# Residual tokens turned on VectorE through HBM, group statistics moved to the second stage, and both ends of the kernel put in a new order

## The reference

```
x1 = x + proj(softmax(q k^T / 16) v),   q, k, v = 1x1 convolutions of group_norm(x, 8 groups)
t  = tokens(x1)                                        # (1024, 256)
a  = ln(t);  u = a / |a|
t2 = t + softmax((u u^T)^2) a                          # second attention, symmetric scores
y  = ln(t2) @ sign(W - mean(W)) * mean|W| + bias
out = t2 + round(clip(y, -1, 1) * 7) / 7               # back to (256, 32, 32)
```

## Time and profile before

| | us |
|---|---|
| median of three runs | 1703.02 (1702.33 to 1707.27) |
| the profiled execution | 1704.85 |
| its span | 1703.1 |
| TensorE matmul busy | 1652.5 (97%) |
| VectorE busy | 1381.0 (81%) |
| ScalarE busy | 989.0 (58%) |
| GpSimd busy | 717.7 (42%) |
| DMA queue, share of 16 engines | 51.1%, 259.48 MB |

### The profile page before, as it was taken

How to read it: one execution, slowest core, us unless ns; L and a number is a source line. 1 busy time by engine, 2 the same in 40 slices (tenths; PEclk the granted TensorE clock), 3 DMA queues, 4 the chain that set the end, 5 groups by cost and what they waited for, 6 DMA issues and landing times.

```text
span 1703.1 us, 33336 instructions
## 1 busy us (share of the span) xinstructions
PE 1652.5 (97%) x10994; PEld 1511.6 (89%) x10994; DVE 1381.0 (81%) x2687; ACT 989.0 (58%) x1586; POOL 717.7 (42%) x1078
## 2 busy tenths in 40 slices
PE   7899999999999999999999999999999999999996
PEld 6798899989899898998989999898998989989895
DVE  7779688787878879788797887878788797887875
ACT  3565655657555565655657566565655656556562
POOL 1262534625345253543625346253542635336251
PEclk9999999999999999999999999999999999999998
DMA  4545546355454554545455463554545545564541
GB/s 144 154 121 170 147 152 184 124 172 158 150 165 143 172 156 151 156 152 185 135 160 161 149 184 124 175 160 146 166 149 174 161 137 155 156 186 107 173 131 56
DMA packets 218750, 259.86 MB, mean 153 GB/s; under 512 B 30176, under 2 KB 188256, under 8 KB 218720
## 3 DMA queue, kind: packets, MB, share of 16 engines
q1 hardware_dynamic: 218720, 259.48, 51.1%
HBM read 138.81 MB, written 120.59 MB: 152 GB/s over the span
## 4 chain that ended last, share of the span: by engine, by line
PE 36%; issue 25%; POOL 15%; DVE 13%; ACT 6%; DMA 2%; SPq 1%; POOLq 1%; DVEq 0%; ACTq 0%
PE wide L466 13%; DVE neg_max L1134 4%; POOL root_pair L1470 3%; PE turn L629 3%; PE turn L631 3%; PE turn L630 3%; PE narrow L629 3%; PE narrow L631 3%; PE narrow L630 3%; PE narrow L466 3%; DVE prob L1206 2%; POOL val L1489 2%; DMA e_scratch<-x_norm 1%; ACT expo L887 1%; DVE x_norm L1143 1%
## 5 line engine op out<-in xcount | busy, mean ns | idle before, releaser
L466 PE MATMUL wide<-xn_hi,prob 128*128 128x512 f32 x1024 | 296.0, 395 | 1.8 <-ACT expo L823 1.1
L823 ACT ACTIVATE expo<-wide,neg_max 128x1024 f32<-128x1024 f32 x128 | 142.9, 1116 | 234.2 <-DVE neg_max L1134 234.2
L466 PEld LDWEIGHTS wide<-xn_hi,prob 128*128 128x128 f32 x1024 | 187.6, 188 | 43.0 <-ACT expo L823 1.2
L1143 DVE STREAM_TRANSPOSE x_norm<-expo 128x1024 f32<-128x1024 f32 x112 | 139.4, 1244 | 51.2 <-ACT expo L823 48.7
L830 ACT ACTIVATE prob<-e_back 128x1024 fp32r<-128x1024 f32 x112 | 118.2, 1055 | 81.1 <-DMA e_back<-e_scratch 80.7
L1513 POOL TENSOR_TENSOR carrier_p<-ones 128x1 f32<-128x1 f32 x60 | 11.7, 195 | 363.5 <-DVE y_sb L1250 361.0
L1497 POOL TENSOR_TENSOR prob<-expo,prob 128x128 fp32r<-128x128 f32 (+6 forms) x112 | 146.7, 1321 | 36.0 <-DVE prob L1183 36.0
L466 PE MATMUL wide<-xn_lo,prob 128*128 128x512 f32 x512 | 160.7, 394 | 0.0
L1134 DVE TENSOR_REDUCE neg_max<-wide 128x1 f32<-128x1024 f32 x128 | 154.3, 1206 | 6.3 <-PE wide L466 6.2
L559 PE MATMUL wide<-prob 128*128 128x256 f32 x512 | 150.3, 294 | 9.0 <-DVE prob L1148 9.0
L1148 DVE TENSOR_TENSOR prob<-e_back,prob 128x1024 fp32r<-128x1024 f32 x112 | 136.0, 1214 | 20.8 <-ACT prob L830 20.3
(11 more groups left out here) (183 smaller groups left out, 5143.2 us busy)
## 6 DMA issues: line engine op xcount, KB each, us to landing
e_scratch<-x_norm SPq DMA_DIRECT2D x112, 512.0 KB, 3.6
e_back<-e_scratch SPq DMA_DIRECT2D x448, 128.0 KB, 3.0
x_raw<-in_x SPq DMA_DIRECT2D x32, 512.0 KB, 3.7
e_back<-in_x SPq DMA_DIRECT2D x64, 256.0 KB, 5.0
out<-y_sb SPq DMA_DIRECT2D x64, 256.0 KB, 3.1
ln_scratch<-x_norm SPq DMA_DIRECT2D x30, 512.0 KB, 3.0
expo<-ln_scratch SPq DMA_DIRECT2D x120, 128.0 KB, 2.9
e_scratch<-x_norm SPq DMA_DIRECT2D x32, 448.0 KB, 2.6
```

Of the source, the lines that this page charges most:

```text
L466: mm = pe.matmul(o, lhsT, r, start=first and i == 0, stop=last and i == len(parts) - 1)
L823: act.activation(expo[:, n % DEEP], wide[n % 2][:, :], ACT.Exp, bias=neg_max[:, n:n + 1], accum_out=row_sum1[:, n:n + 1]).then_inc(e1_made, 1)
L1143: dve.transpose(e_turned[:, n % 2].rearrange("p (q n t) -> p n q t", q=SQ, n=NT), expo[:, n % DEEP].rearrange("p (n q t) -> p n q t", q=SQ ...
```

## The change: what it does

The tokens of the image before no longer go through TensorE in the loop. VectorE turns the squares of `tok` into the space of `ln2` (free by then), SP sends them to a new scratch tensor and fetches them back into the same space, and `output` adds them from there, behind rows 3 and 4 of the second stage. The stores move with it into SP's `second`. The next image's group statistics move from the first to the second stage on all engines. `unit_rows(3)` on ScalarE goes ahead of `square2(3)`. At the start the loads, the first weights, `weight_means` and `signs` are put in another order; at the end `product2(NT - 2)`, `turn_ln2(f, 1)` and `quantise(f, 0)` are. The core of the diff:

```
+        tok_squares = [ln2[:, HT * hf:HT * (hf + 1), :].rearrange("p n c -> p (n c)") for hf in range(2)]
 SP
+            def send_tok(f, hf):
+                sp.wait_ge(tok_turned, 2 * f + hf + 1)
+                sp.dma_start(tok_scratch[hf], tok_squares[hf]).then_inc(tok_written[hf], 16)
+            def fetch_tok(f, hf):
+                sp.wait_ge(tok_written[hf], 16 * (f + 1))
+                back = tok_squares[hf].rearrange("p (q f) -> p q f", q=SQ)
+                for c in range(SQ):
+                    sp.dma_start(back[c * Q:(c + 1) * Q], tok_in[hf, c]).then_inc(tok_landed[hf], 16)
             def second(b, f):
                 send2(b, 0)
+                if f is not None:
+                    store(f, 0)
                 fetch2(b, 0)
                 send2(b, 1)
+                if f is not None:
+                    store(f, 1)
                 send2(b, 2)
...
                 if f is not None:
-                    store(f, 0)
-                    store(f, 1)
+                    for hf in range(2):
+                        send_tok(f, hf)
+                    for hf in range(2):
+                        fetch_tok(f, hf)
 TensorE, front
-                if more:
-                    pe.wait_ge(v_made, 4 * b + 4)
-                    group_means(b + 1)
...
                 scores1(b, 4)
-                if more:
-                    group_vars(b + 1)
-                if f is not None:
-                    pe.wait_ge(y_made, 4 * f + 4)
-                    turn_t(f, 0)
                 product1(b, 0)
                 scores1(b, 5)
-                if f is not None:
-                    pe.wait_ge(out_made, 2 * f + 1)
-                    turn_t(f, 1)
-                if more:
-                    pe.wait_ge(gn_var, b + 2)
                 product1(b, 1)
...
                 scores2(b, 6)
+                if more:
+                    group_means(b + 1)
                 scores2(b, 7)
                 scores2(b, 8)
+                if more:
+                    group_vars(b + 1)
 TensorE, last image
-            for n in range(2, NT - 2):
+            for n in range(2, NT - 1):
                 product2(f, n)
             pe.wait_ge(sq2_made, NP * f + NP)
             turn_ln2(f, 0, LAST)
-            product2(f, NT - 2)
             product2(f, NT - 1)
             ffn(f, 0, LAST)
+            turn_ln2(f, 1, LAST)
             turn_t(f, 0, LAST)
-            turn_ln2(f, 1, LAST)
             ffn(f, 1, LAST)
 ScalarE, front
                 layer_norm1(b, 3)
+                unit_rows(b, 3)
                 square2(b, 3)
                 exp2(b, 3)
-                unit_rows(b, 3)
 VectorE
+            def tok_turn(f, hf):
+                dve.wait_ge(t2_made, NT * f + HT * (hf + 1))
+                for k in range(KC):
+                    last = dve.transpose(
+                        tok_squares[hf].rearrange("p (c k n t) -> p k n c t", c=SQ, k=KC, t=Q)[:, k],
+                        tok[:, HT * hf:HT * (hf + 1), tile(k)].rearrange("p n (c t) -> p n c t", t=Q))
+                last.then_inc(tok_turned, 1)
+            def output(f, hf):
+                dve.wait_ge(tok_landed[hf], 16 * SQ * (f + 1))
+                dve.wait_ge(q_made, 2 * f + hf + 1)
+                y = y_sb[:, hf].rearrange("p k (q f) -> p k q f", q=SQ)
+                dve.tensor_tensor(y, tok_squares[hf].rearrange("p (q k f) -> p k q f", q=SQ, k=KC), y, ALU.add
+                                  ).then_inc(out_made, 1)
 VectorE, front (gn_sums, gn_deviation, gn_variance and output are gone from the first stage)
                 row_max(b, 4)
+                if f is not None:
+                    tok_turn(f, 0)
                 e1_turn(b, 4)
...
                 e1_turn(b, 6)
+                if f is not None:
+                    tok_turn(f, 1)
                 row_max(b, 7)
...
                 cosT_lo(b, 1)
+                if more:
+                    gn_sums(b + 1, 0)
                 residual1(b, 7)
                 cosT_lo(b, 2)
+                if f is None:
+                    signs()
                 e2_turn(b, 1)
+                if more:
+                    gn_sums(b + 1, 1)
...
                 e2_turn(b, 3)
+                if f is not None:
+                    output(f, 0)
                 cosT_lo(b, 3)
                 e2_hi(b, 4)
                 e2_turn(b, 4)
+                if f is not None:
+                    output(f, 1)
                 e2_hi(b, 5)
                 e2_turn(b, 5)
+                if more:
+                    gn_deviation(b + 1)
                 e2_hi(b, 6)
                 e2_turn(b, 6)
+                if more:
+                    gn_variance(b + 1)
 VectorE, last image
             clip(f, 0)
+            quantise(f, 0)
             ln2T_lo_last(f, 1, LAST)
-            quantise(f, 0)
-            output(f, 0, LAST)
+            output_last(f, 0, LAST)
```

More of the change, by code:

```diff
@@ L445, in _ @@
             reload_quads(1)
-            second(0)
+            second(0, None)
             with sp.Fori(1, B - 1) as b:
@@ L450, in _ @@
                 reload_quads(b + 1)
-                second(b)
+                second(b, b - 1)
             front(B - 1, B - 2)
-            second(B - 1)
+            second(B - 1, B - 2)
             store(B - 1, 0)
@@ L467, in three, with query_weights @@
                 return mm
+            def query_weights(k):
+                pe.wait_ge(qkv_loaded, 16)
+                for o in range(KC):
+                    mm = pe.matmul(wide[0][:, k * C:(k + 1) * C], qkv_ld[:, o, tile(k)], qkv_ld[:, KC + o, :],
+                                   start=o == 0, stop=o == KC - 1)
+                if k == KC - 1:
+                    mm.then_inc(prep_pe, 1)
             def prepare():
-                pe.wait_ge(qkv_loaded, QKV_LOADS)
+                pe.wait_ge(proj_loaded, 16)
                 for j in range(KC):
@@ L475, in prepare @@
                 mm.then_inc(prep_pe, 1)
[L477 to L480, removed]
                 pe.wait_ge(gn_var, 1)
+                pe.wait_ge(qkv_b_loaded, 16)
                 for k in range(KC):
@@ L683, in ffn, with turn_t @@
                 mm.then_inc(y_up, 1)
-            def turn_t(f, hf, places=PLACES):
+            def turn_t(f, hf, places):
                 for k in range(KC):
@@ L698, in front @@
                 if f is None:
-                    pe.wait_ge(prep_dve, 8)
+                    weight_sums()
                 queries(b, 1)
                 if f is None:
-                    pe.wait_ge(prep_dve, 12)
+                    pe.wait_ge(prep_dve, 10)
                 else:
@@ L1010, in back @@
                     layer_norm2(b, n)
-            act.wait_ge(prep_pe, 1)
+            normalise(0, 0, False)
+            act.wait_ge(prep_pe, 2)
             act.activation(projT, turn[:, 0:KC * C].rearrange("p (t c) -> p t c", c=C), ACT.Copy
                            ).then_inc(prep_act, 1)
-            for k in range(KC):
-                normalise(0, k, False)
-                norm_hi(0, k, False)
+            norm_hi(0, 0, False)
+            normalise(0, 1, False)
+            norm_hi(0, 1, False)
             act.wait_ge(ffn_loaded, FFN_LOADS)
             act.activation(abs_w, ffn_ld, ACT.Abs, accum_out=w_sum[:, 1:2]).then_inc(prep_act, 1)
-            act.wait_ge(prep_dve, 4)
+            act.wait_ge(prep_dve, 5)
             front(0, None, True)
@@ L1259, in quantise, with output_last @@
                                   ).then_inc(q_made, 1)
-            def output(f, hf, places=PLACES):
-                dve.wait_ge(tT_up, 2 * f + hf + 1)
+            def output(f, hf):
[4 more added lines that the diff above has]
+                                  ).then_inc(out_made, 1)
+            def output_last(f, hf, places):
+                dve.wait_ge(tT_up, hf + 1)
                 dve.wait_ge(q_made, 2 * f + hf + 1)
@@ L1270, in front @@
                 if f is None:
-                    dve.wait_ge(prep_dve, 9)
+                    dve.wait_ge(prep_dve, 8)
                     dve.transpose(quad_bias[:, :, :], out_bias[:, :].rearrange("p (cb cc) -> p cb cc", cc=Q)
                                   ).then_inc(quad_bias_made, 1)
-                    signs()
-                if more:
-                    gn_sums(b + 1, 0)
+                    weight_means()
                 query_lo(b, 0)
@@ L1294, in front @@
                 value_lo(b, 3)
-                if more:
-                    gn_sums(b + 1, 1)
                 if f is not None:
@@ L1303, in front @@
                 row_max(b, 3)
-                if more:
-                    gn_deviation(b + 1)
                 e1T_lo(b, 0)
@@ L1310, in front @@
                 row_max(b, 4)
-                if more:
-                    gn_variance(b + 1)
                 if f is not None:
-                    output(f, 0)
+                    tok_turn(f, 0)
                 e1_turn(b, 4)
@@ L1321, in front @@
                 residual1(b, 1)
-                if f is not None:
```

(18 more changed lines are left out.)

60 lines of the change are left out of this document (37 added, 23 removed).

## The result

The changed kernel takes 1752.04 us (median of 4 runs, 1749.37 to 1755.35) against 1702.67 before (4 runs): a ratio of 1.0285, 95% interval 1.0267 to 1.0304. Slower, as forecast, by 49 us where the forecast said 37.

The account below looks back on a forecast made before the run. TensorE was taken as nearly gapless in the loop, with VectorE's ordered work behind its two due places. Images 1 to 14 +38.5, image 15 +2.4, ends -3.7: +37.2, forecast 1740 us; own range 1725 to 1752, 8 in 10 1680 to 1758.

Parts of the forecast that it names:

- What bounds the kernel: In the loop: TensorE runs nearly without a gap, so an instruction taken from it pays only where nothing else is due.
- First stage: Up to `turn_last_e1`: 0.75 us arrives at `e1_turn(6)`, `tok_turn(f, 1)` adds 1.22, so 0.47 later; net +0.05 an image.
- The bound of the same paragraph: First stage, upper bound: +0.9 us an image if GpSimd's `layer_norm1(0)` is held by `e1T_lo(3)`.
- `unit_rows(3)` first: Second stage: `turn_cos(3)` no longer waits (-0.54 us); `e2_hi(3)` starts at 821.25 instead of 819.98.
- `output(f, 0)`: Second stage, ahead of `cosT_lo(3)`: held by GpSimd's `e2_lo(3)`, `scores2(6)` starts 1.5 us later; not held, 0.5.
- `output(f, 1)` and the port chain: Second stage, rows 4 to 6: begins 1.6 us later, plus 1.1 for `output(f, 1)`: +2.7 an image, at block (1, 0).
- `gn_deviation` (0.75, small operands) fits beside `e2_lo(5)`: Second stage, rows 4 to 6: VectorE's `gn_deviation`, 0.75 us, fits beside GpSimd's `e2_lo(5)`.
- SP's stores, the traffic: Second stage: `fetch2(b, 0)` lands some 5 us later, covered; 2 MB more an image falls into 802 to 815: nothing.
- Ends: First image -1.2 us, `signs` in its second stage +0.8, last image -3.3; together -3.7.
- A: Second stage: VectorE's new work fits its gaps and GpSimd does not hold it; +5.4 us, 1708; chance 0.16.
- B: Loop: `tok_turn(f, 1)` and both `output` lie in waits, TensorE keeps all: 1660 us, half 1682; chance 0.22 with its half.
- C: Ahead of `scores2(6)`: TensorE idles over 2 us, lower clock costs 1.7 an image, 24 more: 1764 us; chance 0.10.

Follow-up runs that it names:

- Run 2: Changed kernel with `tok_turn(f, 1)` ahead of `e1_turn(6)` on VectorE instead of behind it: 1734.27 us, ratio to before 1.0186.
- Run 6: Changed kernel with `tok_turn(f, 1)` ahead of `e1_turn(6)`, both `output` behind `e2T_lo(5)`, group statistics later, `cosT_hi(3)` ahead of `square2(4)`: 1694.06 us, ratio to before 0.9951.
- Run 8: Changed kernel with `unit_rows(3)` behind `exp2(3)` on ScalarE again, as in the kernel before: 1747.49 us, ratio to before 1.0265.
- run 4: Changed kernel with both `output` right behind `cosT_lo(3)`, ahead of `e2_hi(4)`, on VectorE: 1753.35 us, ratio to before 1.0296.
- Run 3: Changed kernel with TensorE's `group_vars` behind the blocks of rows 2 and 3 of `products2_end` instead of ahead of all: 1745.81 us, ratio to before 1.0254.

## Why the prediction was right, and where it was off

- *The number.* 1752.04 lies on the upper edge of the forecast's own range (1725 to 1752) and inside the wide one (to 1758).
- *What bounds the kernel.* Right: TensorE's 1.66 us bought nothing by itself, because VectorE's and ScalarE's chains end together with it. Runs 2 and 6 show it best.
- *First stage.* Here a term of the sum failed: "I take 0.75 for what arrives at `e1_turn(6)`". 0.05 arrived, and `turn_last_e1` came 1.2 later (27.14 to 28.30), not 0.47. The bound of the same paragraph, GpSimd's `layer_norm1(0)` "held by `e1T_lo(3)`, which now falls beside it", is what happened, and it could have been read from the rows: with `output(f, 1)` (1.27) gone from between, `e1T_lo(3)` starts 1.23 instead of 2.41 behind the statistics of `residual1(1)`, while `ln_shift` starts 1.65 behind them. That is 9.7 of the 11.7 that were missing. `product1(1)` waits besides, 1.06, as TensorE comes there earlier than row 1 through HBM; it is part of the 1.66 that were given up as lost.
- *`unit_rows(3)` first.* The chain was right: -0.54 at `turn_cos(3)` and a later `e2_hi(3)` (20.82 behind `turn_last_e1` instead of 20.08, where 1.27 was forecast). Run 8 gives nothing for the net in an undisturbed image.
- *`output(f, 0)`.* Right: held by `e2_lo(3)`, it is 2.04 long, and `scores2(6)` starts 24.65 behind `turn_last_e1` instead of 23.57, 1.08 later (forecast 1.5; the wait is 1.92, since TensorE gets there earlier). Both `output` end 1.09 behind the GpSimd instruction that began before them (846.39, 850.12), and in run 4, with GpSimd idle, each takes 1.22. The Trainium skill, "SBUF — State Buffer", section "Who interferes with whom", has the rule that the later of two such instructions is held for the whole of the other. These ends agree with it.
- *`output(f, 1)` and the port chain.* The size was right (from `turn_last_e1` to the next `ffn(f, 1)` the image shown lost 2.6 and the median image 2.3; the forecast, less the 0.42 of `product1(6)`, is 2.3), the place wasn't: not at block (1, 0) but 1.92 at `scores2(6)` and about 1.6 at `group_vars` (1.16, and an estimated 0.4 behind it: the next matmul starts 0.47 after its last one, and 0.11 in run 3, where it does not wait), less the two old waits. "`gn_deviation` (0.75, small operands) fits beside `e2_lo(5)`" was wrong: it has two inputs in SBUF like the rest and was held, and the forecast did not ask who waits for it. Run 3 shows why that hardly changed the sum: the wait that the forecast priced stands right behind the one that it overlooked. That the one took the other's place at nearly the same price was luck. In image 15, which has no next statistics, TensorE does wait at block (1, 0), 1.32.
- *SP's stores, the traffic.* No wait of TensorE shows them, as forecast. That no engine waits for a transfer from 802 to 815 was misread: ScalarE waits 3.31 for landed rows there (at 805.71). The traffic did no harm at that place, for after the change the same wait is 1.97.
- *Ends.* -2.3 and -4.5 against -1.2 and -3.3; what `signs` costs in its new place can't be told apart in the traces.
- *Rivals.* A (no port) is ruled out by `output` at 2.1; B by the waits; C came in a few images.

## What to carry to other kernels

Work taken off the busiest engine is worth what the chains of the other engines let it be worth: before counting it, look for the next instruction of that engine which has no slack, and ask what makes that one ready. When work is moved beside an engine whose instructions hold its own, price it with the hold of both, in both directions, small operands too, and look for the stretch where that engine idles: here moving the same two instructions into it was worth 35 us. And an instruction that comes earlier than before can be worth less, if its neighbour is now in its way.

## What the runs showed of the hardware that I had not expected

The hold does not depend on size: 2 elements a partition (`gn_d`, 0.16 us alone) waited 0.94 for GpSimd's 1.83 us instruction, and GpSimd's `ln_shift`, as small, waited 0.64 for VectorE's 1.22. In run 4 a chain of three such small instructions ran into the hold at its second member, so being there first with one instruction reserves nothing for the next. And not every pair holds: GpSimd's `root_pair` (128x4, 1.02 us) was still running when `e1T_lo(3)` began at 814.37, and `e1T_lo(3)` took its usual 1.22; 28 more `e1T_lo` of that trace began so and took as long. The rule that held for `output` does not cover them; what is different about `root_pair` no run here tells.
